# An adaptive layer in FP32 on one Trainium2 core: conditional tiles in pairs, buffers in another order, seventh-step splits later

## What is computed

```python
w = weight[adapter_ids]                                  # (8, 1024, 1024)
xc = jnp.einsum('bsi,boi->bso', x, w)
probs = softmax(xc @ W_router.T)                         # 8 experts
combine = top-2 of probs, divided by their sum
h = jnp.einsum('nd,erd->ner', xc, A_stack) * combine[..., None]
lora_out = jnp.einsum('ner,eor->no', h, B_stack) * 2.0
out = x + xc @ W_base.T + b_base + lora_out
```

## Time and profile before

| | us |
|---|---|
| median of 3 runs | 399.78 (399.42 to 399.96) |
| profiled execution | 400.54 |
| its span of instructions | 398.7 |
| PE busy | 391.8 (98%) |
| PE weight loads busy (beside the matmuls) | 332.3 (83%) |
| DVE busy | 302.0 (76%) |
| ACT busy | 183.9 (46%) |
| moved by DMA | 72.96 MB |

### The profile page before, as it was taken

One profiled execution on the slowest core, in us unless ns is written; L12 is line 12 of the kernel. 1 busy time (PEld: TensorE's weight loads), 2 busy tenths in 40 slices (PEclk: granted clock), 3 DMA queues, 4 the chain that ended last, 5 costly groups with the idle time before them and its releaser, 6 DMA issues.

```text
span 398.7 us, 5684 instructions
## 1 busy us (share of the span) xinstructions
PE 391.8 (98%) x2184; PEld 332.3 (83%) x2184; DVE 302.0 (76%) x430; ACT 183.9 (46%) x281; POOL 39.9 (10%) x67
## 2 busy tenths in 40 slices
PE   7999999999999999999999999999999999999996
PEld 6788878888888888888888888888888888888885
DVE  3897876788799999964548787668868999997311
ACT  4786743758632445221146666257656224441000
POOL 0101100101000040011162000000000003101110
PEclk9999999999999999999999999999999999999999
DMA  7988791777530056476569977257084003632222
GB/s 234 369 315 312 282 353 58 251 251 265 185 105 0 29 183 188 157 258 215 193 217 366 354 230 264 96 165 230 27 264 156 5 0 111 197 117 79 81 79 79
DMA packets 21227, 72.96 MB, mean 183 GB/s; under 512 B 2832, under 2 KB 2848, under 8 KB 21200
## 3 DMA queue, kind: packets, MB, share of 16 engines
q1 hardware_dynamic: 15984, 56.11, 40.5%
q0 software_dynamic: 4928, 15.97, 11.4%
q10 hardware_dynamic: 288, 0.52, 0.4%
HBM read 64.20 MB, written 8.39 MB: 182 GB/s over the span
## 4 chain that ended last, share of the span: by engine, by line
PE 85%; DMA 5%; DVE 5%; ACT 2%; SPq 1%; issue 0%
PE bank_x L779 22%; PE bank_x L783 11%; PE bank_y L764 9%; PE bank_y L765 9%; PE bank_y L766 9%; PE bank_x L764 8%; PE bank_x L765 8%; PE bank_x L766 8%; DMA raw<-w_cond 4%; DVE wc_hl L521 3%; PE bank_y L823 2%; ACT wc_hl L459 2%; DMA raw<-x 1%; SPq L350 1%; DVE xp L664 1%
## 5 line engine op out<-in xcount | busy, mean ns | idle before, releaser
L779 PE MATMUL bank_x<-x_hl,wc_hl 128*128 128x512 f32 x512 | 129.0, 393 | 2.1 <-ACT wc_hl L477 2.1
L521 DVE TENSOR_TENSOR wc_hl<-raw,wc_hl 128x1024 fp32r<-128x1024 f32 x90 | 108.8, 1220 | 22.9 <-ACT wc_hl L459 22.9
L459 ACT CAST wc_hl<-raw 128x1024 fp32r<-128x1024 f32 x90 | 94.2, 1053 | 64.8 <-PE bank_y L766 35.0
L779 PEld LDWEIGHTS bank_x<-x_hl,wc_hl 128*128 128x128 f32 x512 | 92.1, 189 | 19.2 <-ACT wc_hl L477 2.7
L783 PEld LDWEIGHTS bank_x<-x_hl,wc_hl 128*128 128x128 f32 x512 | 70.1, 190 | 5.2
L783 PE MATMUL bank_x<-x_hl,wc_hl 128*128 128x256 f32 x512 | 71.7, 282 | 0.0
L411 POOL DMA_DIRECT2D out<-out_sb x28 | 15.3, 546 | 251.7 <-DVE out_sb L572 230.0
L564 DVE SCALAR_TENSOR_TENSOR out_sb<-bank_x,bias_sb,out_sb 128x512 f32<-128x512 f32 x32 | 23.5, 746 | 20.8 <-PE bank_x L766 15.4
L493 ACT CAST xc_hl<-xp 128x256 fp32r<-128x256 f32 x64 | 26.0, 406 | 25.0 <-DVE xp L664 24.9
L765 PE MATMUL bank_x<-x_hl,wc_hl 128*128 128x512 f32 x96 | 37.4, 390 | 0.0
L764 PE MATMUL bank_x<-x_hl,wc_hl 128*128 128x512 f32 x96 | 37.4, 390 | 0.0
(11 more groups left out here) (86 smaller groups left out, 479.0 us busy)
## 6 DMA issues: line engine op xcount, KB each, us to landing
raw<-w_cond SPq DMA_DIRECT2D x62, 512.0 KB, 4.7
raw<-w_base SPq DMA_DIRECT2D x24, 512.0 KB, 5.4
out_sb<-x POOLq DMA_DIRECT2D x32, 256.0 KB, 5.4
raw<-x SPq DMA_DIRECT2D x15, 512.0 KB, 5.1
out<-out_sb POOLq DMA_DIRECT2D x28, 256.0 KB, 2.3
raw<-w_cond SPq DMA_DIRECT2D x4, 256.0 KB, 5.0
out<-out_sb SPq DMA_DIRECT2D x4, 256.0 KB, 2.0
raw<-x ACTq DMA_DIRECT2D x2, 256.0 KB, 2.8
```

What stands on the lines that cost most here:

```text
L459: nc.scalar.copy(split_dst(key, HI), split_src(key)).then_inc(hi_done, 1)
L521: nc.vector.tensor_tensor(split_dst(key, LO), split_src(key), split_dst(key, HI).bitcast(F32), ALU.subtract).then_inc(lo_done, 1)
L779: nc.tensor.matmul(ps[:], wc_hl[:, slot_of(s, t), HI, k], x_hl[:, s % 2, k].rearrange("p h n -> p (h n)"), start=(k == 0), stop=False)
```

## The change

The conditional tiles are taken in lists: in even sequences (0,1), (2,3), (4,5), (6,7), in odd ones (0,1), (2,3), (4,5), (6), (7). For a pair PE does the wide matmuls of both tiles first, then the narrow ones of both. `bias_sb`, `const_sb` and `wr_sb` move behind the large tensors. In odd sequences the splits of step 6 are done together with those of step 7, behind both works on tile 7.

```diff
@@ -65,6 +65,9 @@
 START_STEPS = [(0, 0, 4), (1, 0, 4), (0, 4, 8), (1, 4, 8)]
 WARM, WARM_N = 24, 2 * P
 
+
+COND_TILES = [[(0, 1), (2, 3), (4, 5), (6, 7)], [(0, 1), (2, 3), (4, 5), (6,), (7,)]]
+
 RESIDENT = {(0, 5): [("a", 0, 0)], (2, 5): [("b", 0, 0)]}
 
 
@@ -91,6 +94,13 @@
     if s % GSEQS == GSEQS - 1 and t >= 4:
         items = items + [("T" if t < 6 else "S", s // GSEQS, (P1, t % 2))]
     return items
+
+
+def late_splits(s, t):
+
+    if t < KT - 2 or s % 2 and t < KT - 1:
+        return []
+    return step_splits(s, KT - 2) + step_splits(s, KT - 1) if s % 2 else step_splits(s, t)
 
 
 def slot_of(s, t):
@@ -215,14 +225,15 @@
         a_hl = sb("a_hl", [P, 2, KT, P], F32R)
         b_hl = sb("b_hl", [P, 2, KT + HT, P], F32R)
 
-        wr_sb = sb("wr_sb", [P, KT, NR])
-        bias_sb = sb("bias_sb", [P, KT])
-        const_sb = sb("const_sb", [P, C_ALL])
         out_sb = sb("out_sb", [P, OUTS, PTOK])
         xc_low = sb("xc_low", [P, 2, TOK])
         h_sb = sb("h_sb", [P, PTOK])
         h_hl = sb("h_hl", [P, 2, 2, PTOK], F32R)
         gate_er = sb("gate_er", [P, NQ, EXPERTS, RANK])
+        warm = sb("warm", [P, WARM_N], F32R)
+        wr_sb = sb("wr_sb", [P, KT, NR])
+        const_sb = sb("const_sb", [P, C_ALL])
+        bias_sb = sb("bias_sb", [P, KT])
         logit_sb = sb("logit_sb", [P, NQ, NR])
         logit = logit_sb[:, :, 0:EXPERTS]
         shifted = sb("shifted", [P, NQ, EXPERTS])
@@ -233,7 +244,6 @@
         above = gate_er[:, :, :, 0:EXPERTS]
         equal = gate_er[:, :, :, EXPERTS:2 * EXPERTS]
         stat = sb("stat", [P, 5, NQ])
-        warm = sb("warm", [P, WARM_N], F32R)
 
         ident = const_sb[:, C_ID:C_ID + P]
         before = const_sb[:, C_TRI:C_TRI + EXPERTS * EXPERTS].rearrange("p (e j) -> p e j", e=EXPERTS)
@@ -492,9 +502,8 @@
                         act.wait_ge(xc_summed, c)
                         nc.scalar.copy(xc_hl[:, t, HI, s % 2 * TOK:(s % 2 + 1) * TOK],
                                        xp[:, s // 2 % 2, t, s % 2 * TOK:(s % 2 + 1) * TOK]).then_inc(xc_hi, 1)
-                        if t >= KT - 2:
-                            for key in step_splits(s, t):
-                                hi(key)
+                        for key in late_splits(s, t):
+                            hi(key)
                         if s % GSEQS == 2 and t == 2:
                             h_high(2 * g)
                     if s % GSEQS == 1:
@@ -646,8 +655,8 @@
             for key in START[STARTS:]:
                 lo(key)
 
-            def split_step(s, t):
-                for key in step_splits(s, t):
+            def split(keys):
+                for key in keys:
                     if key[0] == "bd":
                         b_raw = raw[:, LANDED["b", 0, 0][0]]
                         n = HT * P
@@ -664,13 +673,12 @@
                         nc.vector.tensor_tensor(xc, bank_x[t % HT][:, 0:TOK], xc_low[:, t % 2], ALU.add) \
                             .then_inc(xc_summed, 1)
                         if t < KT - 2:
-                            split_step(s, t)
+                            split(step_splits(s, t))
                         dve.wait_ge(xc_hi, c)
                         nc.vector.tensor_tensor(xc_hl[:, t, LO, s % 2 * TOK:(s % 2 + 1) * TOK], xc,
                                                 xc_hl[:, t, HI, s % 2 * TOK:(s % 2 + 1) * TOK].bitcast(F32),
                                                 ALU.subtract).then_inc(xc_lo, 1)
-                        if t >= KT - 2:
-                            split_step(s, t)
+                        split(late_splits(s, t))
                         if s % GSEQS == 2 and t == 2:
                             gate_h(2 * g)
                         if s % GSEQS == 2 and t == 3:
@@ -797,18 +805,21 @@
                     if b == KT:
                         mm.then_inc(cond_done, 1)
 
-            def cond(s, t):
-                pe.wait_ge(hi_done, SPLIT["w", s, t])
-                if t == 0:
-                    pe.wait_ge(lo_done, SPLIT["x", s, 0])
-                    pe.wait_ge(lo_done, SPLIT["x", s, 1])
-                ps = cond_bank(s, t)
-                for k in range(KT):
-                    wide(ps, s, t, k)
-                pe.wait_ge(lo_done, SPLIT["w", s, t])
-                for k in range(KT):
-                    mm = narrow(ps, s, t, k)
-                mm.then_inc(cond_done, 1)
+            def cond(s, tiles):
+
+                for t in tiles:
+                    pe.wait_ge(hi_done, SPLIT["w", s, t])
+                    if t == 0:
+                        pe.wait_ge(lo_done, SPLIT["x", s, 0])
+                        pe.wait_ge(lo_done, SPLIT["x", s, 1])
+                    ps = cond_bank(s, t)
+                    for k in range(KT):
+                        wide(ps, s, t, k)
+                for t in tiles:
+                    pe.wait_ge(lo_done, SPLIT["w", s, t])
+                    for k in range(KT):
+                        mm = narrow(bank_x[t % HT], s, t, k)
+                    mm.then_inc(cond_done, 1)
 
             def router(p):
 
@@ -894,13 +905,12 @@
 
             for g in range(GROUPS):
                 for s in range(GSEQS * g, GSEQS * (g + 1)):
-                    for t in range(KT):
-                        if s == 0 and t < 2:
-                            if t == 0:
-                                first_cond()
-                            continue
-                        cond(s, t)
-                        if s % GSEQS == 2 and t == 1:
+                    for tiles in COND_TILES[s % 2]:
+                        if s == 0 and tiles[0] == 0:
+                            first_cond()
+                        else:
+                            cond(s, tiles)
+                        if s % GSEQS == 2 and tiles[0] == 0:
                             gate_to_rows(2 * g)
                     if s % 2:
                         router(s // 2)
```

## The result

| | before | after |
|---|---|---|
| median, us | 399.66 (399.42 to 399.96, 6 runs) | 401.38 (400.83 to 401.63, 6 runs) |
| ratio | | 1.0039, 95% interval 1.0027 to 1.0051 |
| profiled execution and its span | 400.54, 398.7 | 400.83, 399.0 |
| PE busy | 391.8 | 392.1 |

What follows compares the result with a forecast made beforehand. TensorE bounds the kernel, busy 391.8 of 398.7 us; -0.54 - 1.4 - 0.58 + 2.1 = -0.4 us gives a span of 398.3, as a median 399.3 us, range 398.1 to 401.2.

Steps and rivals of the forecast that it cites:

- Step 1: Order of the conditional matmuls: 27 changes from narrow to wide fall away at 0.02 us each, saving 0.54 us.
- Step 2: LoRA-up matmuls: with `h_hl` at a multiple of 64 bytes, 32 banks save 0.045 us each, 1.4 us.
- rival B: Moving buffers is worth nothing and the wait for weights (3,3) stands: +1.0, so 400.8 us, slower; chance 0.18.
- Step 3: Router of sequence 1: moving a weight split behind tile 7's sum removes a PE wait, saving 0.58 us.
- Step 4: Sequence 2 into 3: pairs delay the ACT and DVE chain; PE waits once for weights (3,3), costing 2.1 us.
- rival D: Clock falls to 1.2 GHz behind the wait, or a second wait opens elsewhere: +2 to +3, 402 us; chance 0.05.

Runs made afterwards that it cites:

- experiment 25: The last experiment (25 counts changes saved): the changed kernel with tiles 2 and 3 of sequences 2 and 3 taken one by one; 397.95 us, ratio 0.9953.

## Why the prediction was wrong, step by step

**Step 1, the order: right.** The kernel with nearly single tiles in sequences 2 and 3 saves 21 changes and needs 0.41 us less work than the buffers alone, that of the last experiment 25 and 0.48: 0.02 us a change, as put. A pair's period after is 5.57 us (97.14 to 102.71), as put.

**Step 2, the buffers: right,** in size (1.4) and cause. The lines of 16 bytes of the Trainium skill (SBUF — State Buffer, Specifications (TRN2)), which rival B took to speak against it, don't tell of this cost: a start 16 or 32 bytes past a multiple of 64 is a multiple of 16, and both cost.

**Step 3, the late splits: right in the profile, wrong as a steady gain.** Four kernels here have the old splits and single tiles, and in their traces the stretch from the router of sequence 1 to the LoRA-down takes 2.49 us (before), 1.89 (buffers alone), 2.29 (`h_hl` 32 bytes late) and 1.88 (16 bytes late); the cast of weights (2,0) waits for its load for 1.27, 0, 1.05 and 0.35 us. So the 0.58 us hang on when one load lands and are in some executions only. With the buffers alone the late splits bring nothing. The term should have stood between 0 and 0.6 and not at 0.58. What the late splits do is protect the pairs: without them two routers take 1.26 us longer each, so inside the change they are worth 2.5 us.

**Step 4, the wait: right** in place, cause and length. Forecast 1.98 and 2.1 with the hand-over; measured 1.86 of idle time, 2.02 from where the next matmul would have started (91.71 less 87.85 + 1.84). There is none in sequence 7, as put.

**The step that failed: the price of that wait.** Step 4 and the sum charged 2.1 us for it and nothing for TensorE's clock behind it. The prediction had the fall in rival D as one of two ways of going wrong, at 2 to 3 us and with 0.05 for both together, since no row showed such a fall. But the trace of before has no idle time of PE over 1.2 us and could not speak against it either. Measured, it is 3.49 - 1.81 = 1.68 us in the trace, and the mean clock is as low in every execution of the changed kernel.

For work in the two traces, where the router's 0.6 us count, the corrected sum is -0.54 - 1.4 - 0.58 + 2.0 + 1.7 = +1.2 us; measured +1.21. For the medians it is +1.8 without the router's part and +1.2 with it. Measured is +1.72, but its interval (1.1 to 2.0 us) holds both, so that the 0.58 us were no part of the median of before is likely and not shown. The clock is the larger error, by far. By itself it lifts the forecast to 401.0 us, still inside the range; the 0.4 us from there to 401.38 are of the size of step 3's error and of the noise.

## What to carry to other kernels

Where TensorE is the bound, price a new wait twice: for itself, and for a stretch at half clock behind it, which here cost nearly as much again behind 1.86 us of idle time. Filler matmuls in the wait, or a small change of the order that halved it, got the second part back. When work is taken in larger bundles, shift the chains that hang on its results by what the bundle delays them, and compare with the slack of each: the place and length of the wait came out of that to a tenth of a microsecond. Mind where a moving operand starts: small tensors go behind the large ones, so that they shift none of these off its multiple of 64 bytes. And count a stall seen in one trace as a sure gain only if other executions have it.

## What was not expected of the hardware

- The granted clock fell to 1.2 GHz behind an idle time of TensorE of 1.86 us, in the traces of the changed kernel and of the pairs alone; the mean clock of 0.996 says the same of all six and of three of four of their executions. It cost about 1.7 us. Behind 0.91 us and, in the start, behind 1.59 us the traces show no fall.
- A moving operand of 512 columns that starts 32 or 16 bytes past a multiple of 64 costs 45 or 57 ns for three matmuls, part of it on the matmuls behind them that have other operands. Starts of the matmuls show it in full, their durations don't.
- Behind narrow matmuls (256 columns) the next five wide ones are slower, 0.03 us altogether: from start to start they take 233, 236, 228, 233 and 231 ns (medians of the trace of before), and then 227. Behind the operand that starts 16 bytes late the slowness ends almost alike, with 231, 236, 228, 232 and 231 ns. What it consists of stays open.
